# Two attention stages in one kernel: low-rank product made once, work moved to ScalarE and GpSimd, another order of work

## The chip, the cores and the metric

One core of one Trainium2 chip runs the whole program. The metric is the device time of one execution in microseconds (us). The five engines have queues of their own, each worked through in order: TensorE (PE), VectorE (DVE), ScalarE (ACT), GpSimd (POOL) and SyncE (SP), which here issues the transfers of the attention stages. They are tied together by semaphores only.

## What is computed

The reference is a stack of six residual blocks on 16 x 256 tokens of width 128. The change touches the two attention blocks:

```
x = x + 0.5 * ffn0(layernorm(x))
x = x + attn0(layernorm(x), Wqa, Wqb, Wkva, Wkvb, Wout, bout)     # 16 heads of 8, low rank, rotated, causal
x = x + 0.5 * ffn0(layernorm(x))
x = x + 0.5 * moe1(layernorm(x))
x = x + attn1(layernorm(x), Wqkv, bqkv, Wout, bout)               # 16 heads of 8, window of 128
x = x + 0.5 * moe1(layernorm(x))

q  = rope(x @ Wqa @ Wqb);  k, v = (x @ Wkva @ Wkvb) split;  k = rope(k)      # attn0
out = softmax(q @ k.T * scale, masked) @ v;   return out @ Wout + bout
```

## The kernel before

One class, `Attention`, makes both attention stages; its flag `low` is true for the first one (called the low stage here) and false for the second (the full stage). Each goes through 16 batches of 256 tokens. The work on one batch is cut into named items, and the items are spread over six pipeline stages: `(3, "nat", 2)` in the list `LOW_ORDER` or `FULL_ORDER` says that in step t the item `nat` 2 is done for batch t - 3. A step goes through the whole list once; 21 steps make one attention stage, nine of them in a loop. Every engine walks the same list (`walk`) and does its own part of an item, so the list is the order of instructions on each engine, SP's queue included.

The items of a batch, in the order in which data goes through them:

- `x`: normalise 256 tokens (DVE). `xT`: transpose them (PE) and copy (ACT). `low`, `proj`: two matrix products and their copies out of PSUM, in the full stage `proj` alone. The copy of `proj` goes to `r0`.
- `rope`: rotation, low stage alone, six DVE instructions from `r0` to `r1`.
- `split`: queries and keys are split into three bf16 parts each, the queries in `qs` by DVE, the keys in `ks` by POOL. Item `split` 0 begins with a cast of the first query part.
- `stk`: SP transposes `ks` into `kT` (item 0) and `qs` into `qT` (item 1), two transfers each. POOL copies the values (item 0). There are three `kT` and `qT` buffers, by batch modulo 3.
- `nat` 0 to 7: scores with queries on the partitions, of which DVE takes the maximum. `max`, `mT`: the maxima are put together (DVE), transposed (PE) and copied (ACT), and SP writes them as rows into `qT` with four small transfers, which count up `attn_mput`.
- `s` 0 to 7: scores with keys on the partitions, minus the maximum, which ACT turns into exponentials; `s` 0 waits for `attn_mput`. In the full stage POOL then cuts the window out.
- `pv` 0 to 3, `evac` 0 and 1, `back`, `norm`, `oT`, `y`, `add`: product with the values, copies, division, output product, and the sum into X with its statistics.

The products of `xT`, `proj`, `s`, `nat` and `back` share three pairs of PSUM banks; each waits until the third one before it has been read. `mT`, `oT`, `y` (and `low`) share one bank.

In SP's part of the code, `stk` first waits until the buffer is free, that is until all eight `s` of the batch three earlier are done (`s_s_ps`), then for the split, then issues its transfers:

```
if name == "stk":
    if self.later(b, 3):
        sp.wait_ge(self.s_s_ps, 8 * (b - 2))
        sp.sem_inc(self.s_go, 1)
    sp.wait_ge((self.s_split_k, self.s_split_q)[a], b + 1)
...
if name == "mT":
    sp.wait_ge(self.s_mrow, b + 1)
```

Between two blocks all engines meet (`ended`): none starts the next one before TensorE, DVE, ACT and POOL have all ended this one.

Of the kernel before, what the change touches and what calls it, by code (L numbers as in the profile page):

```python
# [422 lines left out]
class Attention:  # L423
# [52 lines left out]
    LOW_ORDER = [(2, "split", 1), (5, "s", 7), (3, "nat", 2), (5, "pv", 2), (3, "nat", 3), (3, "nat", 4),  # L476
             (5, "pv", 3), (5, "evac", 1), (1, "proj"), (3, "nat", 5), (2, "stk", 0), (3, "nat", 6), (5, "back"),
             (5, "norm"), (4, "s", 0), (2, "stk", 1), (4, "s", 1), (4, "s", 2), (1, "rope"), (3, "nat", 7),
             (5, "oT"), (4, "s", 3), (3, "max"), (4, "pv", 0), (5, "y"), (5, "add"), (4, "s", 4), (4, "s", 5),
             (4, "pv", 1), (0, "x"), (3, "mT"), (0, "xT"), (1, "split", 0), (4, "evac", 0), (4, "s", 6),  # L480
             (2, "nat", 0), (0, "low"), (2, "nat", 1)]
    FULL_ORDER = [(5, "back"), (5, "norm"), (4, "s", 2), (3, "nat", 6), (3, "nat", 7), (4, "s", 3), (5, "oT"),
             (4, "pv", 0), (4, "s", 4), (1, "rope"), (5, "y"), (4, "s", 5), (0, "x"), (3, "max"), (5, "add"),
             (4, "pv", 1), (3, "mT"), (0, "xT"), (4, "s", 6), (4, "s", 7), (1, "split", 0), (2, "nat", 0),
             (4, "evac", 0), (2, "nat", 1), (2, "nat", 2), (0, "low"), (1, "stk", 0), (2, "nat", 3), (4, "pv", 2),
             (3, "s", 0), (2, "nat", 4), (1, "split", 1), (1, "stk", 1), (4, "pv", 3), (4, "evac", 1), (3, "s", 1),
             (2, "nat", 5), (0, "proj")]
# [18 lines left out]
    def walk(self, eng, fn, ch=None, per=0):  # L506
# [72 lines left out]
    def tensor(self, eng):  # L579
# [4 lines left out]
        def fn(name, a, b, p):  # L584
# [9 lines left out]
            elif name == "low" and self.low:  # L594
# [1 line left out]
                t.matmul(k.PS[0:QL + KVL, 1, 0:S], k.wa[:, :], k.xnT[:, :], start=True,
                         stop=True).then_inc(self.s_low_ps, 1)
            elif name == "proj":
                if self.low:
                    eng.wait_ge(self.s_low, b + 1)  # L600
                else:
                    eng.wait_ge(self.s_xnT, b + 1)
# [968 lines left out]
```

## Time and profile before

| | us |
|---|---|
| median of 3 runs | 1586.96 (1584.87 to 1587.45) |
| the profiled execution | 1589.33, of it span 1587.6 |
| low attention stage | about 185 to 465 of the span |
| full attention stage | about 944 to 1250 of the span |
| PE, DVE, ACT, POOL busy over the span | 76%, 63%, 49%, 37% |

The span is the time from the first to the last instruction in the profile. Instructions have a line of the kernel, and a form (partitions x elements). "Idle before" is time in which the engine had nothing to do, and the name behind the arrow is the instruction whose end released it. The rest of the span is two feed-forward blocks and two expert blocks, whose instructions the change leaves as they are.

### The profile page before, as it was taken

What the parts mean: (1) busy time and instruction counts of PE and PEld (TensorE: products, weight loads), DVE (VectorE), ACT (ScalarE), POOL (GpSimd) and SP (SyncE); (2) the same over time, 40 slices, a digit from 0 to 9 for tenths busy, and PEclk for the clock granted to TensorE, in tenths of its full rate; (3) what the DMA queues carried; (4) which work ended last, traced back from release to release, by engine and by line L of the source; (5) the groups of instructions that cost most, each with busy time, mean ns of one, the idle gap of its engine ahead of it and who ended that gap; (6) DMA issues with size and microseconds to landing.
All of it is one profiled execution on the core that took longest, in us unless ns stands there. A gap on an engine that the chain in (4) does not pass through costs nothing.

```text
span 1587.6 us, 34432 instructions
## 1 busy us (share of the span) xinstructions
PE 1202.7 (76%) x11393; PEld 912.2 (57%) x11394; DVE 997.5 (63%) x1974; ACT 782.1 (49%) x1333; POOL 592.3 (37%) x859
## 2 busy tenths in 40 slices
PE   0677469999956777289999915999997637999992
PEld 0355346666634556278888812455554526888882
DVE  5799589998847995922332357899896373233333
ACT  0444225555554442255555551666666424555556
POOL 2122131221102220056666614676775104666561
PEclk9998669999989896589999956999999757999996
DMA  8000034232300001011111133334232101111115
GB/s 256 8 0 0 1 61 63 44 60 52 51 2 1 0 0 54 1 36 41 42 41 41 40 112 68 69 56 78 57 73 36 54 0 29 42 41 41 40 42 172
DMA packets 161959, 75.58 MB, mean 48 GB/s; under 512 B 126539, under 2 KB 153940, under 8 KB 161876
## 3 DMA queue, kind: packets, MB, share of 16 engines
q1 hardware_dynamic: 152404, 55.06, 15.9%
q0 software_dynamic: 9472, 19.42, 4.1%
q8 instruction: 51, 0.84, 0.2%
q14 instruction: 32, 0.26, 0.1%
HBM read 28.69 MB, written 15.86 MB: 28 GB/s over the span
## 4 chain that ended last, share of the span: by engine, by line
PE 44%; DVE 29%; issue 10%; ACT 8%; POOL 3%; DMA 3%; SPq 1%; DVEq 1%; POOLq 0%; ACTq 0%
PE PS L990 19%; DVE pt L1114 5%; PE PS L656 4%; PE PS L358 2%; ACT xTs L1045 2%; DVE sg L790 2%; PE PS L638 2%; DVE m L790 2%; PE PS L622 2%; PE PS L575 2%; PE PS L950 2%; PE PS L610 1%; ACT pt L1070 1%; SPq L882 1%; DVE q_amax L266 1%
## 5 line engine op out<-in xcount | busy, mean ns | idle before, releaser
L990 PE MATMUL PS<-xTs,pt 128*128 128x128 f32 x2336 | 302.6, 284 | 22.3 <-ACT xTs L1045 7.4
L990 PEld LDWEIGHTS PS<-xTs,pt 128*128 128x128 f32 x2336 | 275.5, 194 | 49.4 <-ACT xTs L1045 49.4
L1114 DVE TENSOR_TENSOR pt<-pt,PS 128x512 f32<-128x512 f32 x146 | 100.4, 688 | 295.4 <-PE PS L990 295.4
L715 ACT ACTIVATE pt<-PS 128x768 f32<-128x768 f32 (+1 forms) x256 | 227.6, 917 | 111.4 <-PE PS L638 59.5
L1227 POOL DMA_INDIRECT xs<-rows,src x152 | 147.3, 969 | 192.4 <-DVE src L1108 146.7
L1236 POOL DMA_INDIRECT outs<-ys,dst x144 | 142.0, 986 | 146.0 <-DVE ys L1122 140.0
L1050 ACT ACTIVATE pt<-PS 128x512 f32<-128x512 f32 x146 | 87.2, 597 | 181.9 <-PE PS L990 181.6
L1039 ACT ACTIVATE pt<-wgu 128x1024 f32 x148 | 156.3, 1057 | 27.3 <-issue 6.9
L790 DVE TENSOR_REDUCE m<-PS 128x4 f32<-128x1024 f32 x128 | 149.2, 1218 | 13.5 <-PE PS L575 12.9
L1010 PE MATMUL PS<-wdn,pt 128*128 x1152 | 152.2, 275 | 0.0
L1010 PEld LDWEIGHTS PS<-wdn,pt 128*128 128x128 f32 x1152 | 140.0, 192 | 0.0
L575 PE MATMUL PS<-tables 64*128 64x128 bf16 (+2 forms) x1536 | 132.2, 252 | 0.0
L790 DVE TENSOR_REDUCE sg<-PS 128x6 f32<-128x768 f32 x128 | 117.6, 953 | 18.9 <-PE PS L575 18.0
L358 PE MATMUL PS<-wguT,xqT 128*128 128x352 f32 x256 | 102.7, 554 | 18.0 <-ACT xqT L403 15.0
L312 POOL TENSOR_TENSOR xhq<-q_mg,fscale 128x256 f32<-128x256 f32 (+1 forms) x32 | 31.5, 1002 | 161.5 <-DVE q_mg L288 156.5
L656 PE MATMUL PS<-pt,v 128*32 128x256 f32 (+1 forms) x1408 | 86.3, 364 | 3.6 <-ACT wraw L721 2.7
L342 PE MATMUL PS<-wdT,hqT 128*128 128x128 f32 (+1 forms) x384 | 54.8, 296 | 44.5 <-ACT hqT L418 44.5
L863 POOL TENSOR_SCALAR_AFFINE_SELECT pt<-pt 128x256 f32<-128x256 f32 x128 | 54.2, 424 | 88.5 <-ACT pt L715 86.0
L358 PEld LDWEIGHTS PS<-wguT,xqT 128*128 128x128 f32 x256 | 55.0, 226 | 54.6 <-ACT xqT L403 27.2
L622 PE MATMUL PS<-kT,qT 64*128 64x128 bf16 (+1 forms) x704 | 68.5, 275 | 19.5 <-DMA qT<-qs 6.9
L342 PEld LDWEIGHTS PS<-wdT,hqT 128*128 128x128 f32 (+1 forms) x384 | 48.4, 202 | 52.9 <-ACT hqT L418 35.8
L575 PEld LDWEIGHTS PS<-tables 64*128 64x128 bf16 x1536 | 73.1, 98 | 7.6
(228 smaller groups left out, 2117.1 us busy)
## 6 DMA issues: line engine op xcount, KB each, us to landing
pt<-outs SPq DMA_DIRECT2D x16, 512.0 KB, 5.0
rows<-qT SPq DMA_DIRECT2D x12, 256.0 KB, 2.4
xs<-rows,src POOLq DMA_INDIRECT x152
outs<-ys,dst POOLq DMA_INDIRECT x144, 2.3
wgu<-in_L_ffn_w_gate SPq DMA_DIRECT2D x1, 2048.0 KB
wgu<-in_L_ffn_w_up SPq DMA_DIRECT2D x1, 2048.0 KB
wdn<-in_L_ffn_w_down SPq DMA_DIRECT2D x8, 256.0 KB
qT<-hqT SPq DMA_DIRECT2D x128, 4.0 KB
```

The lines of the kernel that those rows point to most:

```text
L342: last = t.matmul(k.PS[:, 7, j * D:(j + 1) * D], k.hqT[0:w, j, c, :], k.wdT[0:w, c, :], start=c == 0, stop=c == 2)
L358: last = t.matmul(k.PS[:, bank + j, 0:I0], k.xqT[:, j * P:(j + 1) * P], k.wguT[:, w, :], start=True, stop=True)
L575: last = t.matmul(cols(k.PS[:, self.bank + u, :]), k.eye2[rows, e, :], table[rows], start=False, stop=e == 1, skip_group_check=True)
L656: last = t.matmul(k.PS[32 * u:32 * u + 32, 0, col:col + n], k.v[p][:, kb, g, :], k.pt[:, (2 * a + u // 2) % 4, u % 2, c:c + n], start=kb = ...
L715: s.activation(k.pt[:, a % 4, :, 0:w], k.PS[:, self.bank:self.bank + 2, 0:w], ACT.Exp, scale=self.scale).then_inc(self.s_p, 1)
L790: v.tensor_reduce(out, src, AX.X, ALU.max).then_inc(self.s_nat_read, 1)
L990: last = t.matmul(k.PS[:, 1 + 2 * p + w, c * P:(c + 1) * P], k.wst[:, 1 - p, w, c * P:(c + 1) * P], k.xTs[:, p, :], start=True, stop=True)
L1010: last = t.matmul(k.PS[:, 6, 0:D], k.hs[:, p, c * P:(c + 1) * P], k.wdn[:, ds(e, 1), c, :].squeeze(1), start=c == 0, stop=c == FC - 1)
L1039: s.activation(k.wst[:, 1 - p, :, :], k.wgu[:, :, ds(e, 1), :].squeeze(2), ACT.Copy).then_inc(self.s_wst, 1)
L1114: v.tensor_tensor(k.hs[:, p, :], k.sgs[:, p, :], k.PS[:, 2 + 2 * p, :], ALU.mult).then_inc(self.s_h, 1)
L1227: g.indirect_dma_start(k.xs[:, i % RING, :], None, k.rows[:, :], bass.IndirectOffsetOnAxis(ap=k.src[:, i:i + 1], axis=0)).then_inc(self.s_ ...
L1236: g.indirect_dma_start(k.outs, bass.IndirectOffsetOnAxis(ap=k.dst[:, i:i + 1], axis=0), k.ys[:, u, :], None).then_inc(self.s_st[u], 16)
```

## The change

1. The two low-rank factors are multiplied with each other once, at the end of the first feed-forward block (a transpose, a copy, two products and a copy, on PE and ACT). In the low stage `proj` is then one product of 224 columns for each 128 tokens, and the item `low` is gone.
2. Item `x` moves from DVE to ACT in both stages.
3. The rotation moves from DVE to POOL, with four instructions in place of six.
4. The first cast of the queries becomes an item of its own, `cast`, on ACT in both stages.
5. Both order lists are new, and items change their pipeline stage.

```diff
-             elif name == "low" and self.low:
-                t.matmul(k.PS[0:QL + KVL, 1, 0:S], k.wa[:, :], k.xnT[:, :], start=True,
-                         stop=True).then_inc(self.s_low_ps, 1)
...
-                        t.matmul(k.PS[:, self.bank + j, 0:D], k.low[0:QL, tok], k.wb[0:QL, 0:D], start=True, stop=True)
-                        last = t.matmul(k.PS[:, self.bank + j, D:D + 96], k.low[QL:QL + KVL, tok],
-                                        k.wb[QL:QL + KVL, D:D + 96], start=True, stop=True)
+                        last = t.matmul(k.PS[:, self.bank + j, 0:self.W], k.xnT[:, tok], k.wab[:, :], start=True, stop=True)
...
+            if name == "x":
+                if self.later(b):
+                    eng.wait_ge(self.s_xnT_ps, b)
+                for j in range(2):
+                    i = 2 * (b - self.b0) + j
+                    last = s.activation(k.xn[:, j, :], k.X[:, ds(i, 1), :].squeeze(1), ACT.Identity,
+                                        bias=k.nmr[:, ds(i, 1)], scale=k.rstd[:, ds(i, 1)])
+                last.then_inc(self.s_xn, 1)
...
+            elif name == "cast":
+                eng.wait_ge(self.s_rope if self.low else self.s_r, b + 1)
+                if self.later(b, self.b0 + 1):
+                    eng.wait_ge(self.s_qT, 32 * (b - self.b0))
+                for j in range(2):
+                    last = s.activation(qs[:, j * H:(j + 1) * H, 0:3, :], r[:, j, 0:H, :].unsqueeze(2).broadcast_to([P, H, 3, DH]),
+                                        ACT.Copy)
+                last.then_inc(self.s_cast, 1)
...
+            if name == "rope" and self.low:
+                eng.wait_ge(self.s_r, b + 1)
+                if self.later(b):
+                    eng.wait_ge(self.s_split_q, b)
+                ch.did(g.tensor_tensor(k.rc[:, :, :, :], r0, cs, ALU.mult))
+                ch.did(g.tensor_tensor(k.rs[:, :, :, :], r0, sn, ALU.mult))
+                ch.settle()
+                g.tensor_tensor(rr[:, :, 0::2], rc[:, :, 0::2], rs[:, :, 1::2], ALU.subtract)
+                g.tensor_tensor(rr[:, :, 1::2], rc[:, :, 1::2], rs[:, :, 0::2], ALU.add).then_inc(self.s_rope, 1)
...
+                    nc.tensor.transpose(k.PS[0:QL + KVL, 4, 0:P], k.wa[:, :], k.ident[:, :]).then_inc(s_waT_ps, 1)
+                    pe.wait_ge(s_waT, 1)
+                    nc.tensor.matmul(k.PS[:, 4, P:P + D], k.waT[0:QL, :], k.wb[0:QL, 0:D], start=True, stop=True)
+                    nc.tensor.matmul(k.PS[:, 4, P + D:P + D + 96], k.waT[QL:QL + KVL, :], k.wb[QL:QL + KVL, D:D + 96],
+                                     start=True, stop=True).then_inc(s_wab_ps, 1)
...
-    LOW_ORDER = [(2, "split", 1), (5, "s", 7), (3, "nat", 2), (5, "pv", 2), (3, "nat", 3), (3, "nat", 4),
+    LOW_ORDER = [(4, "s", 5), (5, "y"), (5, "add"), (4, "s", 6), (0, "x"), (2, "nat", 4), (3, "mT"), (4, "s", 7),
```

The first place is SP's queue in the low stage. These rows of before are one step and the beginning of the next: `kT` and `qT` are the transposes of item `stk` (lines L882), `qT<-hqT` the four transfers of item `mT` (L889).

```order
L882 DMA_TRANSPOSE kT_1<-ks 128x4x128 [waits attn_s_ps,attn_split_k]
L882 DMA_TRANSPOSE kT_1<-ks 128x4x128
L882 DMA_TRANSPOSE qT_1<-qs 128x8x128 [waits attn_s_ps,attn_split_q]
L882 DMA_TRANSPOSE qT_1<-qs 128x8x128
L889 DMA qT_0<-hqT 1x8x256 [waits attn_mrow]
L889 DMA qT_0<-hqT 1x8x256 x3
```

And these are SP's rows in the changed kernel, at the same place (L866 is `stk`, L873 is `mT`).

```order
L866 DMA_TRANSPOSE qT_2<-qs 128x8x128 [waits attn_s_ps,attn_split_q]
L866 DMA_TRANSPOSE qT_2<-qs 128x8x128
L866 DMA_TRANSPOSE kT_0<-ks 128x4x128 [waits attn_s_ps,attn_split_k]
L866 DMA_TRANSPOSE kT_0<-ks 128x4x128
L532 UNCONDITIONAL_BRANCH
L532 ISA
L873 DMA qT_1<-hqT 1x8x256 [waits attn_mrow]
L873 DMA qT_1<-hqT 1x8x256 x3
```

The keys' transposes of a batch (`kT`) no longer stand next to the queries' transposes of the same batch; they are the last thing of a step, directly ahead of the maxima's rows of the next step.

The second place is PE's queue in the low stage, from item `mT` to `s` 7 and `nat` 5, in the changed kernel (L619 is `mT`, L628 is `s`, L612 is `nat`, L574 the mask).

```order
L619 MATMUL PS<-identb,hqT 32x128 [waits attn_m,attn_mrow]
L619 MATMUL PS<-identb,hqT 32x128
L628 MATMUL PS<-qT_0,kT_0 128x256 [waits attn_p]
L628 MATMUL PS<-qT_0,kT_0 128x256
L628 MATMUL PS<-qT_0,kT_0 128x128 x2
L574 MATMUL PS<-tables 128x2x64 x2
L574 MATMUL PS<-tables 128x256 x2
L612 MATMUL PS<-q_mg,qT_2 128x128 [waits attn_p]
```

Twenty rows on (behind `nat` 5, `pv` 2, `xT`, `nat` 6 and `pv` 3) come `nat` 7, `s` 0 of the next batch and `proj` (L598).

```order
L612 MATMUL PS<-q_mg,qT_2 128x128 [waits attn_nat_read]
L612 MATMUL PS<-q_mg,qT_2 128x128
L612 MATMUL PS<-q_mg,qT_2 128x256 x2
L574 MATMUL PS<-tables 128x256 x2
L574 MATMUL PS<-tables 128x2x64 x2
L628 MATMUL PS<-qT_1,kT_1 128x256 [waits attn_mput0,attn_xnT]
L628 MATMUL PS<-qT_1,kT_1 128x256
L628 MATMUL PS<-qT_1,kT_1 128x128 x2
L574 MATMUL PS<-tables 128x2x64 x2
L574 MATMUL PS<-tables 128x256 x2
L598 MATMUL PS<-wab,xnT 128x224 [waits attn_xnT,attn_nat_read]
L598 MATMUL PS<-wab,xnT 128x224
```

Before, `s` 0 stood in the step after `mT`, behind `back`, with most of a step between the two (L638 is `s`, L664 is `back`).

```order
L664 MATMUL PS<-ident,wraw 128x128 [waits attn_heads,attn_r]
L664 MATMUL PS<-ident,wraw 128x128 x7
L638 MATMUL PS<-qT_1,kT_1 128x256 [waits attn_mput0,attn_nat_read]
L638 MATMUL PS<-qT_1,kT_1 128x256
L638 MATMUL PS<-qT_1,kT_1 128x128 x2
```

What moved: the last use of buffer `kT_0` by the batch three earlier is `s` 7, which now stands one step later than the `stk` item that waits for it; and from `mT` to the `s` 0 that needs its rows, PE has seven items (`s` 7, three `nat`, two `pv`, `xT`). In the full stage the same distance is `xT`, two `nat`, `s` 7 and `pv` 2, and there `stk` 0 stands behind the `s` 7 that it waits for.

## Rows read from the trace of the kernel before

**Rows 1.** Windows cut where `add` starts: busy us (count) by engine, granted clock, DMA.
```profile
core 0: us, PE busy (x) PEld busy (x) DVE busy (x) ACT busy (x) POOL busy (x), PEclk, DMA share, GB/s
40.00:186.00 146.00, 98.54 (x448) 68.67 (x448) 122.53 (x203) 58.20 (x112) 32.91 (x34) 0.87 0.01 2
185.40:250.39 64.99, 44.24 (x456) 27.68 (x458) 48.22 (x117) 20.13 (x35) 13.86 (x32) 0.68 0.27 50
250.39:417.42 167.03, 159.50 (x2450) 106.37 (x2446) 151.38 (x343) 96.50 (x165) 32.12 (x78) 1.00 0.31 54
417.42:464.92 47.50, 39.70 (x662) 26.43 (x656) 24.25 (x51) 27.13 (x43) 1.42 (x4) 0.98 0.13 20
944.40:1014.94 70.54, 45.26 (x386) 23.90 (x388) 49.62 (x82) 23.25 (x31) 30.52 (x54) 0.71 0.31 57
1014.94:1191.67 176.73, 163.64 (x2048) 92.39 (x2047) 159.69 (x251) 119.10 (x155) 123.48 (x253) 1.00 0.37 68
1191.67:1249.97 58.30, 44.00 (x546) 24.07 (x544) 29.01 (x47) 33.57 (x43) 26.34 (x63) 0.91 0.14 23
```

**Rows 2.** Timeline of PE in one low step: start us, us, line, count.
```profile
313.89 0.67 PE L596 MATMUL PS<-xnT,wa 128*96 128x256 f32 x2
314.49 0.34 PE L622 MATMUL PS<-kT,qT 64*128 64x128 bf16 x4
...
316.41 0.34 PE L622 MATMUL PS<-kT,qT 64*128 64x128 bf16 x4
...
316.75 0.33 PE L622 MATMUL PS<-kT,qT 64*128 64x128 bf16 x4
...
317.18 0.86 PE L656 MATMUL PS<-pt,q_xn 128*32 128x256 f32 x16
317.96 0.48 PE L606 MATMUL PS<-wb,low 64*128 64x128 f32 x2
...
319.57 0.34 PE L622 MATMUL PS<-kT,qT 64*128 64x128 bf16 x4
...
320.50 1.09 PE L664 MATMUL PS<-ident,wraw 128*128 128x128 f32 x8
321.52 0.34 PE L638 MATMUL PS<-qT,kT 64*128 64x256 bf16 x4
```

**Rows 3.** Groups by line and form, whole span, of DVE: count, busy us, mean ns.
```profile
L755 DVE TENSOR_TENSOR rc<-xhq,cos 128x192 f32<-128x192 f32 x32 | 11.2, 351 | 9.8 <-ACT xhq L703 9.8
L770 DVE CAST qs<-r 128x384 bf16<-128x384 f32 x32 | 11.4, 398 | 0.8 <-DMA qT<-qs 0.8
```

**Rows 4.** The same view, of POOL and ACT.
```profile
L830 POOL TENSOR_TENSOR ks<-xhq,gone 128x384 bf16<-128x384 f32 x32 | 26.0, 833 | 23.3 <-ACT xhq L703 18.9 <-DMA kT<-ks 4.4
...
L830 POOL TENSOR_TENSOR ks<-r,gone 128x192 bf16<-128x192 f32 x32 | 15.6, 507 | 115.2 <-DVE r L760 115.2
...
L379 ACT ACTIVATE xh<-X,nmr,rstd 128x128 f32 x20 | 8.7, 484 | 0.0
```

**Rows 5.** Timeline of SP's queue in one low step; "us" is SP's own time.
```profile
313.08 2.70 SPq L889 DMA_DIRECT2D qT<-hqT  x4
316.44 2.51 SPq L882 DMA_TRANSPOSE q_mg<-ks  x2
319.14 2.61 SPq L882 DMA_TRANSPOSE qT<-qs  x2
```

**Rows 6.** Timeline at the end of the full stage: `mT`, its copy, its transfers, `s` 0.
```profile
1226.43 0.28 PE L629 MATMUL PS<-identb,hqT 128*32 128x128 bf16 x2
...
1226.75 0.37 ACT L709 ACTIVATE hqT<-PS 32x256 bf16<-32x256 bf16 x1
...
1227.15 2.67 SPq L889 DMA_DIRECT2D qT<-hqT  x4
...
1231.09 0.61 PE L638 MATMUL PS<-qT,kT 64*128 64x256 bf16 x4 [0.37 <-DMA qT<-hqT]
```

**Rows 7.** Timeline of PE in a full step, from `mT` to `s` 0.
```profile
1080.48 0.28 PE L629 MATMUL PS<-identb,hqT 128*32 128x128 bf16 x2
1080.68 0.44 PE L592 MATMUL PS<-ident,xh 128*128 128x128 f32 x2
...
1083.96 0.38 PE L622 MATMUL PS<-kT,qT 64*128 64x256 bf16 x4
...
1084.43 1.07 PE L656 MATMUL PS<-pt,q_xn 128*32 128x256 f32 x16
1085.44 0.39 PE L638 MATMUL PS<-qT,kT 64*128 64x256 bf16 x4
```

More of the change, by code:

```diff
@@ L474, in __init__ @@
         self.before, self.bank, self.cleared = None, 2, None
-    LOW_ORDER = [(2, "split", 1), (5, "s", 7), (3, "nat", 2), (5, "pv", 2), (3, "nat", 3), (3, "nat", 4),
[L477 to L487, printed above, removed]
+    LOW_ORDER = [(4, "s", 5), (5, "y"), (5, "add"), (4, "s", 6), (0, "x"), (2, "nat", 4), (3, "mT"), (4, "s", 7),
+             (2, "nat", 5), (1, "split", 1), (1, "stk", 1), (0, "rope"), (4, "pv", 2), (0, "xT"), (2, "nat", 6),
+             (4, "pv", 3), (4, "evac", 1), (2, "nat", 7), (3, "s", 0), (0, "proj"), (3, "s", 1), (4, "back"),
+             (4, "norm"), (3, "s", 2), (3, "s", 3), (3, "pv", 0), (2, "max"), (1, "nat", 0), (1, "nat", 1),
+             (0, "cast"), (3, "s", 4), (0, "split", 0), (4, "oT"), (0, "stk", 0), (1, "nat", 2), (3, "pv", 1),
+             (1, "nat", 3), (3, "evac", 0)]
@@ new lines @@
+    FULL_ORDER = [(0, "x"), (5, "add"), (4, "s", 6), (5, "y"), (2, "nat", 1), (3, "mT"), (0, "xT"), (4, "evac", 0),
+             (2, "nat", 2), (4, "s", 7), (2, "nat", 3), (4, "pv", 2), (3, "s", 0), (2, "nat", 4), (1, "stk", 0),
+             (3, "s", 1), (1, "split", 1), (4, "evac", 1), (4, "pv", 3), (3, "s", 2), (2, "nat", 5), (1, "stk", 1),
+             (0, "proj"), (2, "nat", 6), (4, "back"), (3, "s", 3), (3, "pv", 0), (3, "s", 4), (4, "norm"),
+             (3, "s", 5), (2, "nat", 7), (2, "max"), (4, "oT"), (1, "nat", 0), (0, "split", 0), (0, "cast"),
+             (3, "pv", 1)]
@@ L488 @@
     BUFFERED = ("xT", "proj", "s", "nat", "back")
-    SMALL = ("low", "mT", "oT", "y")
+    SMALL = ("mT", "oT", "y")
     STEPS, FIRST, PASSES = B + 5, 7, 3
@@ L495, in read @@
                 "back": (self.s_o, b + 1), "xT": (self.s_xnT, b + 1),
-                "proj": (self.s_r, b + 1), "low": (self.s_low, b + 1), "mT": (self.s_mrow, b + 1),
+                "proj": (self.s_r, b + 1), "mT": (self.s_mrow, b + 1),
                 "oT": (self.s_oT, b + 1), "y": (self.s_added, b + 1)}[name]
@@ L501, in users @@
         for stage, name, *arg in self.ORDER:
-            if name in names and (name != "low" or self.low):
+            if name in names:
                 if not isinstance(t, int) or 0 <= t - stage - self.b0 < B:
@@ L525, in step @@
                     turn += 1
-                elif name in self.SMALL and (name != "low" or self.low):
+                elif name in self.SMALL:
                     if small:
@@ L593, in fn @@
                 last.then_inc(self.s_xnT_ps, 1)
[L594 removed]
+            elif name == "proj":
                 eng.wait_ge(self.s_xnT, b + 1)
[L596 to L602 removed]
                 for j in range(2):
@@ L1358, in __init__, with roped @@
         self.PS = ctx.enter_context(nc.psum_tensor("PS", [P, 8, 512], F32))
+    def roped(self, low, n):
+        if low:
+            return self.r1[:, :].rearrange("p (a h c) -> p a h c", a=2, c=DH)
+        return self.r0[:, :, 0:n * DH].rearrange("p a (h c) -> p a h c", c=DH)
     def sem(self, name):
@@ L1501, in _ @@
                 ph.scalar(act)
+                if i == 0:
+                    act.wait_ge(s_waT_ps, 1)
+                    nc.scalar.activation(k.waT[:, :], k.PS[0:QL + KVL, 4, 0:P], ACT.Copy).then_inc(s_waT, 1)
+                    act.wait_ge(s_wab_ps, 1)
+                    nc.scalar.activation(k.wab[:, :], k.PS[:, 4, P:P + D + 96], ACT.Copy).then_inc(s_wab, 1)
                 ended(act, i)
```

76 lines of the change are left out of this document (25 added, 51 removed).

## Prediction

> **What bounds the kernel now.** I read the times by stage first, with windows cut where the item `add` of a batch starts [rows 1]. From the first to the twelfth `add` the low stage takes 167.0 us, so 11 steps of 15.18; PE is busy for 159.5 us of it, DVE for 151.4. The full stage takes 176.7 us for its 11 steps, 16.07 each, with PE at 163.6 and DVE at 159.7. The reader is to see that both stages are nearly PE-bound, with DVE close behind, ACT at 58% and 67% and POOL at 19% in the low stage, while filling and emptying each pipeline costs over 100 us (65.0 + 47.5 and 70.5 + 58.3). Taking work off PE and DVE aims at the right engines. The second thing read was the timeline of PE inside a low step [rows 2]: from start to start an `s` or `nat` takes 0.34 us, a `pv` 0.78, `back` 1.02, item `low` 0.60 and `proj` 1.61. The third was SP's queue, which looks idle in a summary but is where this change is decided.
>
> **The change part by part.**
>
> *Low-rank product.* Item `low` streams 2 x 256 columns in 0.60 us, 1.17 ns each [rows 2]. The new `proj` streams 4 x 224 = 896 columns, 1.05 us. PE loses 0.60 + 1.61 - 1.05 = 1.16 us a step. The whole PE work of a new low step is 16 x 0.34 + 4 x 0.78 + 1.02 (`back`) + 0.8 (`y`, four products, taken like `pv`) + 2 x 0.4 (`xT`, `oT`, each a quarter of `back` and a change of kind) + 0.2 (`mT`) + 1.05 = 12.4 us; the old one by the same prices is 13.6, and took 15.2, so about 1.6 us of a step are changes of kind and waits. The one-time product at the end of the first block is two transfers through ACT and some 1.2 us of half-clock products; DVE and POOL wait for it at the meeting of the engines: +2 us, once (bounds 1 and 4).
>
> *Rotation, cast, normalisation.* DVE loses six instructions of 0.35 that start 0.27 apart, 1.8 us, and two casts, 0.6 us of new time [rows 3], and two normalisations, 0.6 (two overlapping instructions like them): 3 us of 13.8 in the low stage, about 1.9 of 14.5 in the full one. POOL gets two instructions over 384 columns and two over 192, priced as its own such rows, 2 x 0.83 + 2 x 0.51 = 2.7 us [rows 4]; its low-stage load goes from 2.9 to 5.6 us of a step. The Trainium skill, GPSIMD Engine Reference, section 4.1, says to keep two-input elementwise work on VectorE, GpSimd being about twice as slow; rows say 2.7 against 1.8. Either is hidden: with `proj` copied at 2.2 us after `s` 0, keys rotated at 5 and split at 8, they are ready before SP may fetch them, below. ACT gets 2 x 0.48 for `x` [rows 4] and about 1.0 for the cast, less 0.4 in the low stage: 8.8 + 1.6 = 10.4 us, not a bound. So DVE and ACT would allow steps of 11 and 13 us.
>
> *The new order, low stage.* SP takes its rows in order and each costs it time: 2.51 and 2.61 us for a pair of transposes, 2.70 for the four row transfers [rows 5]. Item `stk` 0 of batch b is now the last of step b. It first waits for all `s` of batch b - 3, and `s` 7 of that batch is an item of step b + 1, one place behind `mT`. The transfers of `mT` of step b + 1 are queued behind it on SP. So when `s` 7 ends, SP first issues the key transposes and only then the rows of maxima, for which `s` 0 on PE waits. Price: 0.2 us until `s` 7 has drained, 0.1, 2.51 for the transposes and 0.2 to the next issue; from there to `s` 0 3.94 us (1227.15 to 1231.09, where `s` 0 was released by just this transfer [rows 6]). Sum 6.9 us from the end of `s` 7 to the start of `s` 0. What PE has between the two is three `nat`, two `pv` and `xT`, 3 x 0.34 + 2 x 0.78 + 0.4 = 3.0 us. The rest of the step, from `s` 0 to the end of `s` 7, is 12.4 - 3.0 = 9.4 us of work, and with 1 us of the gaps that every step has, 10.4. **Step: 10.4 + 6.9 = 17.3 us**, 2.1 more than now, although PE has less to do; it would stand still nearly 4 us in each. Bounds: 16.3 (no gaps) and 18.3 (2 us of them). Queued behind SP's wait are also the query transposes: issued at 9.5 after `s` 7 they land near 10, when PE is still in front of `nat` 0 (about 11.4), so that adds nothing.
>
> The Trainium skill, DMA: Bandwidth & Descriptors, "Anatomy of one DMA", says that a wait is made on the issuing sequencer, not in the DMA engine, which speaks for this blockage. Its table there gives some 50 ns for dispatch, which speaks against its price; the rival "SP costs nothing" below is what would follow. The rows have 0.65 us and 1.25 us for one issue, and I go by them.
>
> Low stage sum. Fill: the first batch's way to `nat` 0 is no shorter, since `kT` and `qT` still go one after the other; `mT` of batch 0 stands behind the key transposes of batch 2 (at 228), so `s` 0 is at 232; `s` 7 at 241 sends the second `s` 0 to 248, and the first `add` comes 9 us later, near 257, against 250.4: +7, in which the 2 us of the one-time product are contained (bounds 0 and +14). Eleven steps: 11 x (17.3 - 15.18) = +23. Emptying: one more step is held (16.3, without `proj`), then about 12.6, 12 and 9, 49.9 against 47.5: +2. Sum **+32 us** (from steps of 16.3 to 18.3: +15 to +50).
>
> *The new order, full stage.* Here `stk` 0 stands behind the `s` 7 it waits for, so SP is free. But `s` 0 has moved up to `mT`: before, 4.96 us lay between their starts (1080.48 to 1085.44 [rows 7]), filled with two `s`, three `nat` and more. Now it is `mT`, `xT`, two `nat` (0.47 each, 1083.96 to 1084.43), `s` 7 (0.33) and one `pv` (1.01, 1084.43 to 1085.44): 0.2 + 0.38 + 0.94 + 0.33 + 1.01 = 2.9 us, against 1231.09 - 1226.43 = 4.66 us [rows 6] for copy, issue and landing. PE's busy 163.6/11 = 14.9 us [rows 1] less 2.9 leave 12.0 for the other part. 12.0 + 4.66 = 16.7, and `mT` also waits for `add` behind `y`, 0.3: **17.0 us a step** against 16.07 (bounds: 15.2, if the maxima arrive in time, and 17.6, if DVE is late for `add`). Eleven steps: +10. Fill: DVE and the transfers set it as before, -1. Emptying: 58.3 now, partly at a lower clock (0.91 [rows 1]); with DVE relieved and the first `add` of a step at its head, four steps of 15, 15, 12 and 10: -6. Sum **+3 us** (-14 to +14).
>
> **The sum.** The profiled execution took 1589.33 us, 1587.6 of it span. +32 + 3 makes 1624 of it; its own time is 2.4 us over the median of the three runs, so 1622 against 1586.96. About 0.2% (3 us) is what a measurement of this kernel can tell from no change.
>
> **The rivals.**
>
> 1. *SP holds nothing, and issues cost nothing: PE-bound, faster.* If SP worked ahead, or the rows of maxima came within the 3 us of PE work, low steps would be 12.4 and 1 us of gaps, 13.4, full ones 15.2. That is 11 x 1.8 + 11 x 0.9 = 30 us, with some 9 us more where pipelines fill and empty, less 2: 1550 us. It decides when the way from `s` 7 to `s` 0 costs under 4.8 us, since 10.4 + 4.8 is the old step. For it: PE and DVE are the present bounds, and both lose work. Against it: the durations in SP's queue [rows 5], which must all be paid one after the other. 14%.
> 2. *SP's order does not matter, but the maxima's own way does.* `mT` then waits on ACT behind `x`, so about 10 us after `s` 0 plus 1 plus 4: steps of 15 us, the low stage as now, full stage as forecast: 1580 to 1592. 8%.
> 3. *The clock falls too.* PE would stand still in each low step. In the feed-forward stage, where it works 98.5 of 146 us, the granted clock is 0.87; through the low steps it is 1.00, at 95% [rows 1]. At 0.87 a quarter of the time is at half speed, and of PE's 10.4 us a step a quarter would be twice as long, +2.6 us, over 12 steps +31 at the most and half of that likelier: 1637 to 1653. 15%.
> 4. *As forecast*, 1600 to 1637. 63%.
>
> **How the numbers follow.** 1622 is the time of the likeliest case. The range leaves out the PE-bound case and half of the second, and reaches into the clock case: 1586 to 1650. Slower by over 0.2%: cases 3 and 4 and a fifth of 2, 0.79. Faster: case 1 and a third of 2, 0.17. Within 0.2%: 0.04.
>
> **What would show it.** The timeline of SP: in each low step a wait that ends at the last matmul of `s` 7, then two transposes and four row transfers without a gap. In PE's waits: `s` 0 of the low stage idle near 4 us, released by DMA `qT<-hqT`, sixteen times; in the full stage the same wait at 1 to 2 us. DVE's busy time per low step near 10.8, PE's near 13. The first `add` at 257, steps of 17.3 and 17.0. I am wrong if the low `s` 0 follows `nat` 7 without a gap, if `s` 7 comes much earlier than 10.4 us after `s` 0, or if SP's issues turn out shorter next to each other than in these rows.

## The result, and the profile after

The changed kernel takes 1671.12 us (median of 4 runs, 1669.68 to 1676.19) against 1587.01 for the kernel before on the same chip: ratio 1.0534, 95% interval 1.0509 to 1.0558. It is slower by 84 us, where 35 were forecast. The profiled execution has a span of 1667.9 us against 1587.6, 80.3 more.

The page of the changed kernel, engines, the chain that ended last, and one group:

```profile
PE 1214.3 (73%) x11302; PEld 914.8 (55%) x11303; DVE 934.4 (56%) x1750; ACT 830.9 (50%) x1447; POOL 642.6 (39%) x923
...
PE 42%; DVE 26%; issue 9%; ACT 8%; SPq 6%; DMA 6%; POOL 2%; DVEq 1%; POOLq 0%; ACTq 0%
...
L628 PE MATMUL PS<-qT,kT 64*128 64x256 bf16 x704 | 68.0, 281 | 54.7 <-DMA qT<-hqT 49.3
```

SP's queue and DMA, 1% and 3% of the chain before, hold 6% each now, and `s` (L628) has 49.3 us of idle time behind the transfers of the maxima. DVE has less to do (it fell from 63% to 56% of the span), PE has fewer matmuls (11302 for 11393) and is busy for longer (1214.3 us for 1202.7), and the waits grew.

The windows of the changed kernel, cut at `add` like [rows 1], with the same columns:

```profile
187.00:260.35 73.35, 44.19 (x484) 27.32 (x486) 36.06 (x66) 28.09 (x53) 30.65 (x54) 0.66 0.25 44
260.35:475.08 214.73, 170.55 (x2384) 110.14 (x2381) 126.76 (x232) 115.28 (x199) 68.17 (x121) 0.88 0.23 42
475.08:525.84 50.76, 39.48 (x592) 25.46 (x590) 19.49 (x44) 26.17 (x40) 0.29 (x1) 0.91 0.09 18
1005.60:1076.60 71.00, 46.53 (x424) 24.98 (x424) 41.79 (x61) 34.03 (x55) 32.56 (x61) 0.76 0.36 61
1076.60:1274.80 198.20, 166.55 (x2046) 93.45 (x2046) 147.44 (x210) 132.29 (x197) 122.28 (x254) 0.97 0.34 60
1274.80:1330.30 55.50, 40.83 (x506) 22.45 (x506) 25.67 (x42) 30.57 (x40) 23.01 (x57) 0.93 0.15 21
```

Beside the rows of before: the 11 low steps take 214.73 us for 167.03, 19.5 a step for 15.2, and the clock in them is 0.88 where it was 1.00. The 11 full steps take 198.2 for 176.7, 18.0 for 16.1. Measured from the phase's own start, the first `add` of the low stage comes 75.8 us in (65.0 before), that of the full stage 71.8 (70.5). Low stage as a whole +61.7 us, full stage +19.9. The two expert blocks and the second feed-forward block differ by 0.3 us at the most, and the first one, at whose end the one-time product stands, is 0.9 us shorter.

PE's timeline in one low step of the changed kernel (L619 is `mT`, L628 `s`, L598 `proj`, L654 `back`), where [rows 2] had no gap:

```profile
357.89 0.29 PE L619 MATMUL PS<-identb,hqT 128*32 128x128 bf16 x2
358.11 0.34 PE L628 MATMUL PS<-qT,kT 64*128 64x256 bf16 x4
...
361.25 0.34 PE L612 MATMUL PS<-q_mg,qT 64*128 64x128 bf16 x4
361.43 0.33 PE L574 MATMUL PS<-tables 64*128 64x256 bf16 x4
365.68 0.34 PE L628 MATMUL PS<-qT,kT 64*128 64x256 bf16 x4 [3.92 <-DMA qT<-hqT]
365.86 0.33 PE L574 MATMUL PS<-tables 64*128 64x128 bf16 x4
366.12 1.45 PE L598 MATMUL PS<-wab,xnT 128*128 128x224 f32 x4
367.49 0.50 PE L628 MATMUL PS<-qT,kT 64*128 64x256 bf16 x4
367.79 0.53 PE L574 MATMUL PS<-tables 64*128 64x128 bf16 x4
368.25 1.92 PE L654 MATMUL PS<-ident,wraw 128*128 128x128 f32 x8
370.10 0.34 PE L628 MATMUL PS<-qT,kT 64*128 64x256 bf16 x4
...
377.64 0.34 PE L628 MATMUL PS<-qT,kT 64*128 64x256 bf16 x4
377.82 0.33 PE L574 MATMUL PS<-tables 64*128 64x128 bf16 x4
```

SP's queue in the same step, against [rows 5]:

```profile
358.86 2.50 SPq L866 DMA_TRANSPOSE kT<-ks  x2
361.79 2.71 SPq L873 DMA_DIRECT2D qT<-hqT  x4
364.84 2.63 SPq L866 DMA_TRANSPOSE qT<-qs  x2
```

`mT` ended at 358.2 and its copy stood ready soon after, but SP first waited for `s` 7 (its products and mask end at 358.6), then issued the key transposes for 2.5 us, and sent the maxima's rows only at 361.79. PE stood still from 361.8 to 365.68, and the next `s` 7 is over at 378.15. The hold is as forecast, step by step. Behind it stands what I had given only 15%: `proj` takes 1.45 us and `back` 1.92 (1.09 in [rows 2]), because PE's granted clock has gone to its lower level behind the idle stretch, and it is back by 370.1. The stretch and what follows it, as windows (the clock is the third number from the end of a line):

```profile
361.70:365.68 3.98, 0.06 (x3) 0.00 (x1) 1.05 (x2) 0.29 (x1) 0.03 (x1) 1.00 0.11 20
365.68:369.00 3.32, 3.32 (x24) 2.24 (x25) 0.00 (x0) 2.00 (x3) 0.70 (x1) 0.64 0.85 158
```

The waits over ten such steps (engine, what waits, for what: us in total, times, longest):

```profile
DVE den L782 <- PE PS L654: 73.5, 10, 7.9
...
PE PS L628 <- DMA qT<-hqT: 36.9, 10, 4.3
```

Not only PE waits. DVE has nothing to do for 7.4 us of each step, until `back` comes.

The full stage, `add`, `mT`, copy, transfers and `s` 0, against [rows 6] and [rows 7]:

```profile
1148.74 0.28 PE L619 MATMUL PS<-identb,hqT 128*32 128x128 bf16 x2 [0.92 <-DVE X L787]
...
1149.15 0.37 ACT L714 ACTIVATE hqT<-PS 32x256 bf16<-32x256 bf16 x1 [1.07 <-PE PS L619]
1149.55 2.70 SPq L873 DMA_DIRECT2D qT<-hqT  x4
...
1153.44 0.39 PE L628 MATMUL PS<-qT,kT 64*128 64x256 bf16 x4 [1.19 <-DMA qT<-hqT]
```

From `mT` to `s` 0 it is 4.70 us (forecast 4.66). What was missed stands in the first row: `mT` itself waits 0.9 us for `add`.

### The profile page after: what moved, and what is told of

It reads as the page before. It is cut to its first block, busy times and chain, and to the rows that moved or that the text cites. A ratio compares the mean times of both kernels' runs of the same rounds, so it can differ in the third digit from the quotient of the medians.

```text
span 1667.9 us, 34171 instructions
## 1 busy us (share of the span) xinstructions
PE 1214.3 (73%) x11302; PEld 914.8 (55%) x11303; DVE 934.4 (56%) x1750; ACT 830.9 (50%) x1447; POOL 642.6 (39%) x923
## 4 chain that ended last, share of the span: by engine, by line
PE 42%; DVE 26%; issue 9%; ACT 8%; SPq 6%; DMA 6%; POOL 2%; DVEq 1%; POOLq 0%; ACTq 0%
PE PS L974 18%; DVE pt L1098 4%; SPq L873 3%; PE PS L628 3%; DMA qT<-hqT 3%; PE PS L646 3%; SPq L866 3%; PE PS L654 2%; ACT xTs L1029 2%; PE PS L358 2%; PE PS L574 2%; DVE m L764 2%; PE PS L612 2%; DVE sg L764 2%; DVE q_amax L266 1%
## 5 line engine op out<-in xcount | busy, mean ns | idle before, releaser
L764 DVE TENSOR_REDUCE m<-PS 128x4 f32<-128x1024 f32 x128 | 153.3, 1220 | 71.8 <-PE PS L574 70.3
L574 PE MATMUL PS<-tables 64*128 64x128 bf16 (+2 forms) x1536 | 138.3, 261 | 0.0
L764 DVE TENSOR_REDUCE sg<-PS 128x6 f32<-128x768 f32 x128 | 117.7, 951 | 26.6 <-PE PS L574 24.1
L628 PE MATMUL PS<-qT,kT 64*128 64x256 bf16 x704 | 68.0, 281 | 54.7 <-DMA qT<-hqT 49.3
L612 PE MATMUL PS<-kT,qT 64*128 64x128 bf16 (+1 forms) x704 | 68.6, 275 | 29.6 <-DMA qT<-qs 19.1
L574 PEld LDWEIGHTS PS<-tables 64*128 64x128 bf16 x1536 | 77.1, 102 | 8.9
```

The source lines that it names most:

```text
L574: last = t.matmul(cols(k.PS[:, self.bank + u, :]), k.eye2[rows, e, :], table[rows], start=False, stop=e == 1, skip_group_check=True)
L628: last = t.matmul(k.PS[:, self.bank + u, c:c + n], k.kT[p][rows, kg, j * P:(j + 1) * P], k.qT[p][rows, a, q0:q0 + n], start=j == 0, stop=j ...
L764: v.tensor_reduce(out, src, AX.X, ALU.max).then_inc(self.s_nat_read, 1)
```

## The experiments

Twelve kernels, grouped by what they ask. Each was timed against the kernel before on its own chip (medians of it 1584.65 to 1587.79 us), so differences between kernels are taken from their ratios, times 1587 us. The tables of order are lists of (stage, item, number).

### The old order with the new placement

Both lists are those of before, without `low`, and with `cast` directly ahead of `split` 0. All else is the changed kernel.

```diff
-    LOW_ORDER = [(4, "s", 5), (5, "y"), (5, "add"), ...
+    LOW_ORDER = [(2, "split", 1), (5, "s", 7), (3, "nat", 2), ...
+                 ... (0, "xT"), (1, "cast"), (1, "split", 0), ...
```

> The changed placement (product made once, normalisation and cast on ScalarE, rotation on GpSimd) with the order lists of before; the item low dropped and cast put directly ahead of split 0. Theory A, the new order alone costs the time: low steps 13.5 to 14.2 us, full steps 15.2 to 15.8, about 1555 to 1570 us, faster than before. Rival B, ScalarE and GpSimd themselves hold the stages back: low steps stay at 15.2 or above, 1590 us or more.

Measured: 1671.92 us, ratio 1.0534 (1.0513 to 1.0555), the same as the changed kernel. Theory A falls: the old order does not bring the time back. But the loss is another one, and rival B, which had 1590 us or more, is left. The low stage is 298.5 us from its start to the last `add` (before 279.5, changed 341.2), the full stage 365.9 (305.5 and 325.4). Timeline of ACT and DVE in a full step of this kernel (L699 is `cast`, L748 the subtraction of `split` 0):

```profile
1147.29 1.94 ACT L720 ACTIVATE pt<-PS 128x1024 f32<-128x1024 f32 x2
...
1149.12 0.93 ACT L699 ACTIVATE qs<-xhq 128x384 bf16<-128x384 f32 x2
...
1150.08 1.12 DVE L748 TENSOR_TENSOR dq<-xhq,qs 128x128 f32<-128x128 f32 x2 [4.60 <-ACT qs L699]
```

DVE stands still for 4.6 us. Its `split` 0 needs the cast, the cast stands in ACT's queue behind two exponentials, and behind DVE's wait are the maxima of the next `nat` items, for which PE then waits: in this kernel's waits, `PE PS L612 <- DVE m L764` has 25.6 us in nine steps. The granted clock is lower too, 0.95 over its low steps and 0.90 over its full ones, where it was 1.00 in both before.

### The key transposes behind the `s` 7 they wait for

```diff
 LOW_ORDER of the changed kernel:
-  (4, "oT"), (0, "stk", 0), (1, "nat", 2)
+  (4, "oT"), (1, "nat", 2)
-  (3, "mT"), (4, "s", 7), (2, "nat", 5)
+  (3, "mT"), (4, "s", 7), (1, "stk", 0), (2, "nat", 5)
```

> The changed kernel, but in the low stage item stk 0 stands one step later, directly behind the s 7 that it waits for, so that the rows of maxima are issued ahead of it. Theory A, SyncE's hold is 7 us of each low step and the half clock behind it another 2: the hold goes, s 0 still waits 1 to 1.5 us for the maxima, low steps near 15 us, 1610 to 1622 us. Rival B, the 2 us over the forecast are waits of the new order, not the clock: low steps near 17, 1635 to 1645 us. Rival C, the hold is no cause: 1665 or more.

Measured: 1650.62 us, ratio 1.0393 (1.0371 to 1.0415). 22 us come back, less than half of what theory A wanted; the time lies between B (1635 to 1645) and C (1665 or more). The waits of this kernel over its 11 low steps (us in total, times, longest) tell why:

```profile
PE PS L612 <- DMA qT<-qs: 19.4, 10, 3.2
PE PS L628 <- DMA qT<-hqT: 17.4, 11, 2.4
```

The maxima's rows no longer stand behind a held queue, and the wait of `s` 0 falls from 36.9 us in ten (changed kernel) to 17.4 in eleven. What stays is the maxima's own way, some 4.7 us with 3.0 us of PE work beside it. And a new wait has come: the queries' transposes are still the last of the three in SP's queue (6.7 us after the end of `s` 7 for 5.9, in the mean of ten), while `s` 0 comes 2.0 us sooner, so now `nat` 0 waits for them. The low step is 17.8 us, and theory A had this wait at nothing.

### `mT` earlier, in one stage and in both

```diff
 low:
-  (2, "nat", 4), (3, "mT"), (4, "s", 7)
+  (2, "nat", 4), (4, "s", 7)
-  (3, "s", 4), (0, "split", 0)
+  (3, "s", 4), (2, "mT"), (0, "split", 0)
 full:
-  (2, "nat", 1), (3, "mT"), (0, "xT")
+  (2, "nat", 1), (0, "xT")
-  (4, "oT"), (1, "nat", 0)
+  (4, "oT"), (2, "mT"), (1, "nat", 0)
```

In the low stage the four transfers then stand ahead of the held key transposes; in the full stage `mT` stands before `add` and has most of a step before `s` 0.

> The changed kernel, but in the low stage item mT stands one step earlier, behind s 4, so its transfers are issued before SyncE is held. The hold stays, and delays the key transposes alone. Theory A, only what s 0 waits for counts: no wait in front of s 0, nat 0 may wait up to 1 us, low steps 13.5 to 14.5 us, clock 1.00 again, 1600 to 1612 us. Rival B, the held key transposes cost as much at nat 0: low steps of 17 or more, 1640 us.

> The changed kernel, but in the full stage item mT stands one step earlier, behind oT, so that it waits neither for add nor does s 0 wait for its transfers. Theory A, those two waits (1.2 and 1.0 us a step) are what makes full steps 18.05 instead of 16: full steps 15.5 to 16.2, 1645 to 1652 us. Rival B, DVE's late maxima hold the stage: full steps 17.3 or more, 1662 to 1671 us.

> Changed kernel with mT a step's part earlier in both stages (the edits of the low and of the full stage measured apart took 52 and 11 us off). If they are independent, as two stages that don't meet should be: 1608, from 1604 to 1612; low step 15.4 to 16.9, full step 17.3. Theory O says the rest to 1587 is waits that the new order still has; theory P says it is the cast and the rotation.

Measured: low stage alone 1619.22 (1.0207, 1.0181 to 1.0233), full stage alone 1659.87 (1.0451, 1.0422 to 1.0480), both 1604.47 (1.0125, 1.0099 to 1.0151). Against 1671, moving one item takes off 52 us, 13 us and 65 us: the two stages add up, as expected. Theory A had 1600 to 1612 for the first and was nearer than B. For the second, A had 1645 to 1652 and full steps of 16.2 at most, B had 1662 to 1671 and 17.3 or more: the time lies just outside B and the step is B's. With `mT` early in the low list alone, the windows of the 11 low steps:

```profile
253.00:429.70 176.70, 154.34 (x2378) 102.55 (x2376) 133.25 (x232) 115.78 (x198) 68.09 (x121) 0.95 0.30 51
```

214.7 us have become 176.7, the clock 0.95, and PE's wait for `qT<-hqT` is gone from the list of waits. The place of this one item carried 38 us in these steps and 8 each in filling and emptying. The low step is now 16.1 us. Part of what stays above the old order is the clock: the five steps with a stretch at the lower level take 16.7 to 17.0 us, the others 15.1 to 16.0. The other part is a wait of PE, for the same item's neighbour: `oT` (L660) writes the bank that `mT` used and waits for its copy (waits of the same kernel and window):

```profile
PE PS L660 <- ACT hqT L714: 16.0, 11, 1.7
```

In the full stage `mT` early takes the clock from 0.97 to 1.00 and the step from 18.0 to 17.3; PE's busy time in the 11 steps falls by 5.4 us (166.6 to 161.2), while the steps get 7.8 us shorter. What PE waits for in these steps is DVE, and ACT's copy of `oT`, on whose bank the early `mT` waits (waits over eleven steps):

```profile
PE PS L628 <- DVE m L764: 12.5, 11, 1.4
PE PS L619 <- DVE hqT L775: 10.5, 7, 1.5
...
PE PS L619 <- ACT oT L732: 6.0, 4, 1.5
```

### Order against placement

Here `x`, the rotation and the first cast are back on DVE; the low-rank product stays in both kernels. One has the new order (with `rope` behind `pv` 0 in the low list), the other the old one.

```diff
 ScalarE:
-            if name == "x":
-            elif name == "cast":
 VectorE:
+            if name == "x":
+            elif name == "rope" and low:
             elif name == "split" and a == 0:
-                eng.wait_ge(self.s_cast, b + 1)
+                for j in range(2):
+                    ch.did(v.tensor_copy(qs[:, j * H:(j + 1) * H, 0:3, :],
+                                         r[:, j, 0:H, :].unsqueeze(2).broadcast_to([P, H, 3, DH])))
 GpSimd:
-            if name == "rope" and self.low:
```

> Changed kernel with its new order, but x, the rotation and the first cast are back on DVE (the rotation item stands behind pv 0 of the low list, since on DVE it can't stand ahead of proj); the low-rank product stays. With it the three kernels measured so far make a table of order against placement. Theory O (the new order's own waits, the maxima's rows behind a held SP queue and s 0 close behind mT, cost the time whatever engine has the work): 1640 to 1700, low step 18 to 20, with the 3 to 4 us wait of s 0 for the maxima's transfers still there in each low step. Theory P (the placement costs it: under the old order the cast on ACT is what DVE waits 3.4 us a step for in the low stage and 4.6 in the full stage): 1590 to 1615.

> The kernel before with one part of the change alone: the low-rank factors multiplied once, the item low gone, old order, x, rotation and cast on DVE. If PE binds the low stage (159.5 us busy of 167.0 at full clock), a step loses up to 1.16 us: 1568 to 1574. If DVE (151.4 of 167.0) or the chain through the buffers takes over at once, a step loses 0.3 us or less: 1580 to 1588. Theory P and O say the same here.

Measured: 1728.84 us with the new order (1.0884, 1.0846 to 1.0922), 1578.01 with the old one (0.9951, 0.9932 to 0.9969). With the first run this is a table, the low-rank product in all four:

| ratio to before | old order | new order |
|---|---|---|
| `x`, rotation, cast on DVE | 0.9951 | 1.0884 |
| on ACT and POOL | 1.0534 | 1.0534 |

Neither theory is right by itself, and the time with the new order is beyond what both expected. The new placement costs 93 us under the old order and gives back 56 under the new one; the new order costs 148 us with the old placement and nothing with the new one. The two fit each other, and are a bad pair all the same. With the new order and the old engines everything of the hold is still there, and since DVE has more to do, its own lateness comes on top (waits of that kernel over ten low steps of 21.7 us):

```profile
PE PS L628 <- DMA qT<-hqT: 35.1, 10, 4.0
...
PE PS L612 <- DVE sg L774: 20.0, 16, 1.9
```

The product alone is worth 8 us (12.5 in the low stage of the profiles), which lies between the two expectations. The windows of the 11 low steps of that kernel:

```profile
244.00:404.00 160.00, 146.41 (x2382) 98.15 (x2380) 150.32 (x342) 93.50 (x154) 32.23 (x78) 1.00 0.32 56
```

A step is 14.54 us for 15.18. PE's busy time fell by 1.19 us a step (1.16 forecast), 0.64 of it reached the time, and DVE is at 94% now.

### One placement at a time, under the old order

Each starts from the kernel with the product alone, 1578.0 us: the rotation on POOL; `x` on ACT in its old place; `cast` on ACT directly ahead of `split` 0; last, rotation on POOL and `x` on ACT, but behind `norm` in both lists, 15 items earlier in the low list and ten in the full one.

```diff
 product, rotation on GpSimd, x on ScalarE and early (low list; the full list alike):
-  (5, "back"), (5, "norm"), (4, "s", 0)
+  (5, "back"), (5, "norm"), (0, "x"), (4, "s", 0)
-  (4, "pv", 1), (0, "x"), (3, "mT")
+  (4, "pv", 1), (3, "mT")
```

> As the kernel with the product alone (old order, x and cast on DVE), and the rotation on POOL. DVE loses 1.9 us a low step; POOL gets 3.3 us (1.00, 1.00, 0.68, 0.69 in the changed kernel). If the rotation on POOL costs nothing, the low step is the shorter of PE's or DVE's: 1560 to 1572, at most that of the product alone. If the queries' split on DVE, behind the longer rotation, becomes late (theory P): 1585 to 1600. The full stage stays as it was.

> The kernel with the low-rank product alone (old order, measured 1578), and item x on ACT in both stages in the old order's place; rotation and cast on DVE. Under the old order with all placements of the change, PE waited 1.2 us a low step and 0.7 a full step for x on ACT (it was 0.3 on DVE before), since x stands behind exponentials there. Theory P, this is a part of the 94 us that the placement costs under the old order: 1590 to 1600. If DVE's 1.2 us are worth more than that wait: 1565 to 1575.

> As the last, with x back on DVE and the first cast of the queries on ACT directly ahead of DVE's split 0, in both stages. Under the old order with all placements DVE waited 3.4 us a low step and 4.6 a full step for it. Theory P, this is most of the 94 us: 1640 to 1665, above all by the full stage (366 us there for 305). If the wait only shows together with the rotation on POOL: under 1610.

> The kernel with product and rotation on POOL in the old order (measured 1576), and x on ACT, behind norm in both lists (some 20 items ahead of its old place), where ACT idled for 1.9 us. Theory P says that a placement costs only by the place that it gets in its new engine's queue: then x on ACT is free here, DVE has 1.2 us a step more, and it is 1570 to 1577, the fastest of all; if x still comes late for xT: 1585 or more.

Measured:

| kernel | us | ratio (95%) | low step | full step |
|---|---|---|---|---|
| product alone | 1578.0 | 0.9951 (0.9932 to 0.9969) | 14.54 | 16.26 |
| + rotation on POOL | 1576.1 | 0.9934 (0.9912 to 0.9955) | 14.46 | 16.09 |
| + `x` on ACT, old place | 1601.1 | 1.0076 (1.0054 to 1.0098) | 16.13 | 16.89 |
| + `cast` on ACT | 1643.8 | 1.0366 (1.0338 to 1.0393) | 15.46 | 20.54 |
| + rotation on POOL, `x` on ACT early | 1576.9 | 0.9940 (0.9924 to 0.9957) | 14.28 | 16.33 |

The cast is 66 of the 93 us and `x` 20; with -3 for the rotation that makes 83 of 93. The cast and the early `x` are inside what was expected of them, `x` in its old place is 1 us above it, and the rotation, put at 1560 to 1572 if it cost nothing, came out at 1576. The rotation on POOL costs nothing, but DVE's 1.9 us are worth next to nothing as well, since PE is the bound: 146.4 us busy of 159.0 in its 11 low steps. The waits of the kernel with the cast (full steps), and of the one with `x` in its old place (low steps; L591 is `xT`):

```profile
DVE dq L746 <- ACT qs L691: 37.3, 10, 3.8
...
PEld PS L612 <- DVE m L776: 32.0, 15, 3.1
```

```profile
PE PS L591 <- ACT xh L686: 12.4, 10, 1.2
```

DVE waits 3.7 us in a full step for two casts that take ACT 0.9 us. `x`, of 0.9 us as well, comes 1.2 us late for `xT`; moved to where ACT idled, it comes in time, and the low step is the shortest of all, 14.28.

The waits are not the whole price; the lower clock behind them is the other part. With `cast` on ACT the 11 full steps have a mean clock of 0.87, and PE is busy for 183.9 us in them, against 163.6 at 1.00 in the kernel before. With `x` in its old place five of the 11 low steps have a stretch at the lower level, and these take 17 us where the six others take 15.4 or 15.5. Here are the full steps of the first kernel, then the first two low steps of the second:

```profile
1020.50:1246.45 225.95, 183.86 (x2048) 98.13 (x2046) 154.48 (x230) 128.00 (x177) 122.36 (x253) 0.87 0.30 53
```

```profile
244.72:261.70 16.98, 14.81 (x224) 9.73 (x220) 13.27 (x31) 9.35 (x16) 2.93 (x8) 0.90 0.26 50
261.70:277.20 15.50, 13.47 (x224) 9.01 (x220) 13.26 (x30) 9.24 (x16) 2.92 (x8) 1.00 0.29 53
```

So of the 1.6 us that the low step grew by with `x` on ACT, about 0.9 are the wait and 0.7 the clock. In the early place the clock is 1.00 through all low steps.

Over the whole kernel the gain of the early `x` is not to be told from the rotation alone or the product alone: the intervals of the three ratios overlap. All three beat the kernel before, by 0.5 to 0.7%, and the changed kernel by 93 to 95 us of medians.

### Products in the wait

The changed kernel with work that nobody reads in the place of PE's idle stretch. It does more work than the changed kernel.

```diff
             elif name == "s":
                 if a == 0:
+                    if self.low:
+                        for _ in range(22):
+                            t.matmul(k.PS[:, self.bank, 0:3 * P], k.identb[:, :], k.causal_s[:, 0:3 * P],
+                                     start=True, stop=True, skip_group_check=True)
                     eng.wait_ge(self.s_mput, 64 * (b - self.b0 + 1))
```

> The changed kernel, with 22 products of 384 columns that nobody reads put ahead of s 0 in the low stage, into the bank that s 0 then overwrites, so that PE doesn't idle while the maxima's rows come. It does more work than the changed kernel; only the clock can make it faster. Theory C (the half clock behind the wait is a cost of its own, 11 steps at a mean clock of 0.88 are some 4.7 us a step at half clock, up to 2.3 us lost): low step 19.5 becomes 17.2 to 18.5, 1640 to 1656. If the half clock costs nothing because others wait anyway: 1671 or more.

Measured: 1655.94 us, ratio 1.0431 (1.0414 to 1.0448), 15 us less than the changed kernel (1671.12). Windows of its 11 low steps, and PE in one of them (L625 are the added products, L632 is `s`):

```profile
262.30:461.80 199.50, 189.13 (x2620) 119.85 (x2618) 131.43 (x232) 114.38 (x198) 68.28 (x121) 1.00 0.26 45
```

```profile
375.73 3.58 PE L625 MATMUL PS<-tables,identb 128*128 128x384 bf16 x21
379.24 0.34 PE L632 MATMUL PS<-qT,q_mg 64*128 64x256 bf16 x4
...
379.67 1.02 PE L598 MATMUL PS<-wab,xnT 128*128 128x224 f32 x4
...
381.06 1.09 PE L658 MATMUL PS<-ident,wraw 128*128 128x128 f32 x8
...
390.03 0.34 PE L632 MATMUL PS<-qT,q_mg 64*128 64x256 bf16 x4
```

The clock is 1.00 through all low steps, `proj` takes 1.02 us for 1.45 and `back` 1.09 for 1.92, and the step is 18.1 us for 19.5. From the end of `s` 7 to `s` 0 it is as long as in the changed kernel (6.8 us for 6.9 in the mean); only what comes behind it is faster. So the lower clock cost 1.4 us a step, 15 us in all, and theory C holds, at the upper edge of its range. PE's waits for DVE's maxima are still there in this kernel:

```profile
PE PS L612 <- DVE sg L768: 9.6, 20, 0.8
```

## Why the prediction was right in sign and too small

1. **The hold in SP's queue: right.** From the end of `s` 7 to `s` 0 it is 7.1 us in the step shown (358.6 to 365.68) and 6.9 in the mean, forecast 6.9, and PE's wait is 3.9, "nearly 4". Moving `mT` alone ahead of the hold takes 52 us away, moving the held transposes 22.
2. **From `s` 0 to the end of `s` 7: the term that was mis-sized.** The sum put "9.4 us of work, and with 1 us of the gaps that every step has, 10.4". Measured are 12.5 us (365.68 to 378.2), 12.0 of them busy. The run with products in the wait divides the 2.1 us. At full clock the same stretch is 11.3 us (379.24 to 390.5), and PE is busy for 10.4 of them: as PE's work at full clock the term was right. The sum had two things at nothing. One is the half clock: it makes PE's work in this stretch 1.6 us longer, hides some of the waits, and costs 1.4 us a step. The other is DVE: with the clock at 1.00 PE still idles for 0.9 us of the stretch, nearly all of it in waits for DVE's maxima (9.6 us in some 11 steps of that kernel; in the changed one, where PE is slower, 3.3 us in ten). That DVE is late because it starved while PE stood still is my reading of these waits, and was not tested by itself.
3. **The clock: a rival that should have been a term.** I held case 3 against case 4 as alternatives, 15% to 63%, with "half of" +31 us. Both happened together: with the forecast stall filled, the clock stays up, so the fall comes with the stall. Its price, 15 us, is what I had put, with some luck: the 0.87 behind the +31 was the clock of another stage (here it is 0.88), and "half of that likelier" had no working. Forecast plus this term is 1637. Of the other 34 us, 15 lie in the rest of the low stage (points 2 and 4) and 17 in the full stage (point 5).
4. **Low stage, fill and end.** +10.8 and +3.3 us where +7 and +2 were put. With +47.7 for the 11 steps (forecast +23) it is +61.7 for +32. At the end it is the held step that was put too short, 18.9 us for 16.3.
5. **Full stage.** `mT` to `s` 0: 4.70 us for 4.66, right. "And `mT` also waits for `add` behind `y`, 0.3" is 1.0 us (11.5 us in eleven steps): `add` stands behind `split` 0 on DVE, and so does everything of PE behind `mT`. "12.0 for the other part" was PE's busy time with no gap at all, and became 12.3, since PE also waits for DVE's maxima (5.8 us in ten). 0.7 and 0.3 make 18.0 us a step, where the sum had 17.0. That the emptying would save 6 us: it saved 2.8. Together +19.9 us for +3. The early `mT` gives back 0.7 of the step, with the clock back from 0.97 to 1.00. The other 1.2 above 16.1 was not tested; in that kernel PE waits 1.1 us a step for DVE's maxima and 1.5 at `mT`, for DVE's row of maxima and for the copy of `oT`.
6. **The rotation on POOL "is hidden": right.** It takes 3.4 us there (1.00, 1.00, 0.68, 0.69) where 2.7 were put from rows of another form, and costs nothing, as measured under the old order: ratio 0.9934 with it, 0.9951 without. The Trainium skill, GPSIMD Engine Reference, section 4.1, has GpSimd at about twice VectorE's time; here it is 3.4 us in four instructions for 1.8 in six, which agrees, and it did not decide anything.
7. **"So DVE and ACT would allow steps of 11 and 13 us": the view that was wrong.** Loads said nothing of it. ACT had room, and the cast on it cost 66 us under the old order. (DVE's relief was also put too high: 3 us of a low step and 1.9 of a full one, where its busy time fell by 2.2 and 1.1; the terms named for the full stage, casts 0.6 and normalisations 0.6, add up to 1.2.) I had costed the casts and `x` by their durations, and not by what stands ahead of them in ACT's queue and behind them in DVE's. That this did not spoil the forecast is luck: under the new order the same three moves gave back 56 us. It also means that the order is not the cause by itself: with the old order and these engines the same 84 us are lost, in other waits and at a lower clock.
8. **The product: +2 us once, and "PE loses 1.16 us a step".** The one-time part is not to be seen: the first block is 149.6 us long in the profile of before, and 147.2 to 151.1 in the thirteen with the product. Of 1.16 us, 0.64 came through when it was the only change.

The experiments do not settle why the new order, at its best here (1604), still stays 28 us above the old one with the product alone; `oT` behind `mT`'s copy is 1.5 us of each low step, four of the 11 low steps still have a stretch at the lower clock, and in the full stage there are the waits of point 5.

## What to carry to other kernels

An engine's spare time doesn't say that an item can go there: ask what stands ahead of it in that queue, and who waits behind its reader. The same item, `x` on ACT, cost 20 us in one place of the list and nothing in another; the cast of 0.9 us, behind two exponentials, cost 66, and the lower clock behind the waits is part of both prices. Order and placement are one edit: each of the four pairs must be costed, and a part that is simply less work (here the product) should be measured by itself, since it was the only gain clear of noise and drowned in the rest.

In a queue such as SP's here, a transfer whose data is due soon should not stand behind one that waits for a buffer; moving one item ahead of it gave back 52 us. And where a stall of PE is forecast in each step, put the lower clock behind it into the sum, and the waits of the engines that starved meanwhile.

## What the runs showed of the hardware

PE's granted clock went to the lower level of 1.2 GHz (half of 2.4) in the middle of a steady stage, behind an idle stretch of only 3.9 us in the step shown, and in each of the 11 low steps (0.88 in the mean), although PE was 79% busy over them. With 3.6 us of unread products in the same stretch it stayed at 2.4 GHz through all steps (1.00 over 199.5 us). So work that nobody needs made the kernel 15 us faster. In the kernel with the early `mT`, whose longest waits of PE are 1.7 us, five low steps still have a stretch at the lower level, and so have five with `x` in its old place on ACT, where the longest are 1.2 us; with `cast` on ACT the longest are 1.4 us and no low step has one. I can't say from these rows what sets them off.

The Trainium skill, DMA: Bandwidth & Descriptors, "Anatomy of one DMA", has some 50 ns for dispatch, in a table that its heading gives to transfers issued by GpSimd; the prediction read it as one for SP. SP's rows in this kernel are 2.71 us for four row transfers and 2.50 for two transposes, one behind the other without overlap.
